# FFN's last 42 inner channels in one output product instead of three, in a one-core attention and FFN kernel

## The reference, cut to what matters

```python
HID = int(DIM * 4 * 2 / 3)          # 682 with DIM = 256
h = shift_token(x)
h = (h - mu) / jnp.sqrt(var + 1e-05) * lg + lb
h = h @ w1 + b1                     # 2 * 682 columns
a, g = jnp.split(h, 2, axis=-1)
h = a * jax.nn.gelu(g, approximate=False)
x = x + h @ w2 + b2                 # 682 rows of w2
```

## Time and profile before

| | |
|---|---|
| median of 3 runs | 1422.95 us (1420.28 to 1424.81) |
| profiled execution, its own time | 1424.29 us |
| its span in the trace | 1422.5 us |
| TensorE busy | 1374.8 us, 97% |
| TensorE weight loads | 1050.5 us, 74% |
| VectorE busy | 963.8 us, 68% |
| ScalarE busy | 878.1 us, 62% |
| GpSimd busy | 762.1 us, 54% |
| chain that ended last | PE 78%, ACT 11%, DVE 5%, issue 4% |

### The profile page before, as it was taken

The page is one execution under the profiler, slowest core; times in us unless marked ns, Lnnn a source line. Parts: engine busy times, 40 slices in busy tenths (PEclk is TensorE's granted clock), DMA queues, the critical chain, the costliest instruction groups (busy, mean ns, idle before and its releaser), DMA issues.

```text
span 1422.5 us, 24115 instructions
## 1 busy us (share of the span) xinstructions
PE 1374.8 (97%) x7740; PEld 1050.5 (74%) x7740; DVE 963.8 (68%) x2671; ACT 878.1 (62%) x2223; POOL 762.1 (54%) x522
## 2 busy tenths in 40 slices
PE   6999997999999999999999999999999999999988
PEld 5878775777777777777777777786777777777756
DVE  6877765767676666666667777676767676766657
ACT  4556656575747575747475766666565757575763
POOL 2425765564647373738373747464655646473710
PEclk9999999999999999999999999999999999999998
DMA  7111100000000000000001010000000000000046
GB/s 220 38 51 60 55 30 1 1 1 0 0 0 0 0 0 0 0 0 0 0 1 60 14 47 1 1 0 0 0 0 0 0 0 0 0 0 0 0 145 210
DMA packets 35243, 33.33 MB, mean 23 GB/s; under 512 B 8364, under 2 KB 32896, under 8 KB 35200
## 3 DMA queue, kind: packets, MB, share of 16 engines
q1 hardware_dynamic: 35200, 32.79, 7.3%
HBM read 24.39 MB, written 8.39 MB: 23 GB/s over the span
## 4 chain that ended last, share of the span: by engine, by line
PE 78%; ACT 11%; DVE 5%; issue 4%; POOL 1%; DMA 0%; ACTq 0%; SPq 0%; DVEq 0%; POOLq 0%
PE l_psF L1399 9%; PE l_psP L842 9%; PE l_ring L842 9%; PE l_ring L1399 8%; PE l_ring L1469 7%; ACT l_att L1073 7%; PE l_psP L1453 6%; PE l_psF L1487 6%; PE l_psS L1410 5%; PE l_psS L1422 4%; PE l_ring L653 3%; PE l_psF L1439 2%; PE l_psS L671 1%; PE l_psP L688 1%; ACT L1163 1%
## 5 line engine op out<-in xcount | busy, mean ns | idle before, releaser
L955 POOL TENSOR_TENSOR l_att<-l_att 128x1024 f32<-128x1024 f32 x64 | 153.1, 2403 | 315.7 <-DVE l_att L880 315.7
L1007 POOL TENSOR_TENSOR l_att<-l_att,l_rinv 128x1024 f32<-128x1024 f32 x64 | 126.4, 1975 | 70.7 <-DVE l_rinv L1243 70.4
L1053 ACT ACTIVATE l_att<-l_psP 128x384 f32<-128x384 f32 (+1 forms) x128 | 70.3, 549 | 120.7 <-PE l_psP L1453 120.4
L1248 DVE COPY l_att<-l_psP 128x384 f32<-128x384 f32 (+1 forms) x128 | 78.9, 617 | 86.7 <-PE l_psP L1453 82.5
L1453 PE MATMUL l_psP<-ident,l_att 128*128 128x128 f32 x896 | 124.5, 279 | 2.0 <-DVE l_att L1248 1.5
L1453 PEld LDWEIGHTS l_psP<-ident,l_att 128*128 128x128 f32 x896 | 98.6, 141 | 32.4 <-issue 28.2
L962 POOL TENSOR_TENSOR l_att<-l_att,l_rn 128x1024 f32<-128x1024 f32 x64 | 120.8, 1910 | 0.7 <-ACT l_rn L861 0.5
L1073 ACT ACTIVATE l_att<-l_psF,l_nb 128x256 f32<-128x256 f32 x256 | 118.1, 483 | 2.1 <-DVE l_nb L1236 2.1
L971 POOL TENSOR_TENSOR l_u_lo<-l_att,l_u_hi 128x512 fp32r<-128x512 f32 x75 | 95.7, 1288 | 39.1 <-ACT l_u_hi L1048 39.0
L1469 PE MATMUL l_ring<-l_att 128*64 128x256 f32 (+1 forms) x1024 | 112.5, 362 | 2.0 <-ACT l_att L1053 1.4
L1236 DVE CUSTOM_DVE_ANT_0 l_psF<-l_psF,w_mask 128x256 f32<-128x256 f32 x256 | 101.1, 456 | 16.3 <-issue 16.3
(11 more groups left out here) (209 smaller groups left out, 4037.2 us busy)
## 6 DMA issues: line engine op xcount, KB each, us to landing
a_tables<-in_x SPq DMA_DIRECT2D x8, 512.0 KB, 4.3
scratch_s<-a_o SPq DMA_DIRECT2D x8, 512.0 KB, 3.2
l_att<-in_x SPq DMA_DIRECT2D x8, 512.0 KB, 8.8
l_att<-scratch_s SPq DMA_DIRECT2D x8, 512.0 KB, 9.0
out_dram<-l_att SPq DMA_DIRECT2D x7, 512.0 KB, 7.8
aw_stage<-in_wqkv SPq DMA_DIRECT2D x2, 768.0 KB, 5.9
l_att<-in_wqkv SPq DMA_DIRECT2D x2, 768.0 KB, 5.4
w_w_raw<-in_w SPq DMA_DIRECT2D x2, 640.0 KB
```

The costliest lines, as they stand in the source:

```text
L955: pool.tensor_tensor(rot[:, t, :], rot[:, t, :], t2[t % 2], ALU.add).then_inc(S["added"], 1)
L1007: pool.tensor_tensor(pr, pr, along(inv, 2 * P), ALU.mult).then_inc(S["p_done"], 1)
```

## The change

Tile 5 of the FFN has only 42 inner channels, and its operands have 128 rows. The change fills the rows with the parts of the split, so that one product gives all three. With AGAIN = 10 (channels 32 to 41), the rows are, for the hidden values: 0 to 41 high parts; 42 to 51 and 52 to 61 channels 32 to 41 again, as low and as high parts; 64 to 95 low parts of channels 0 to 31; 96 to 127 high parts of channels 0 to 31 again. The rows of w2 are laid out to match (high, high, low; high; low). The columns of w1 and the entries of b1 for channels 32 to 41 are loaded two more times, so that the hidden product itself makes the copies.

```diff
 load_w1, for each half s:
+            for r in range(2):
+                c1 = c + HREM + r * AGAIN
+                sp.dma_start(stage[:, :, c1:c1 + AGAIN], w1[:, :, (s + 1) * HID - AGAIN:(s + 1) * HID]).then_inc(self.S["w1_in"], 16)
 load_w2:
-        sp.dma_start(self.w2_raw[0:HREM, HFULL, :], self.io["w2"][layer, HFULL * P:HID]).then_inc(self.S["w2_in"], 16)
+        for p0, first, n in ((0, 0, HREM), (HREM, 32, AGAIN), (HREM + AGAIN, 32, AGAIN), (64, 0, 32), (96, 0, 32)):
+            row = HFULL * P + first
+            sp.dma_start(self.w2_raw[p0:p0 + n, HFULL, :], self.io["w2"][layer, row:row + n]).then_inc(self.S["w2_in"], 16)
 load_small:
+        sp.dma_start(self.less[:, :], io["fless"]).then_inc(small, 16)
 and for each layer l and half s:
+                for r in range(2):
+                    p0 = s * GATE0 + HREM + r * AGAIN
+                    sp.dma_start(self.b1col[p0:p0 + AGAIN, l, 2 * HFULL:W1T], rest[32:HREM], allow_slow_non_contiguous=True).then_inc(small, 16)
 low_w2 covers tiles 0 to 4 only; new:
+    def end_w2(self, dve, layer):
+        end = (slice(0, P), HFULL)
+        dve.wait_ge(self.S["small"], self.SMALL)
+        dve.wait_ge(self.S["w2_hi"], layer + 1)
+        dve.scalar_tensor_tensor(out=self.w2_hi[end], in0=self.w2_hi[end].bitcast(F32), scalar=self.less[:, 1:2], in1=self.w2_raw[end],
+                                 op0=ALU.mult, op1=ALU.add).then_inc(self.S["w2_end"], 1)
 ScalarE, u_high (gelu and gated now cover rows 0 to 63 instead of 0 to 41):
+            if j == HFULL:
+                act.activation(U_hi[96:P, j, :], gate_of(j, attn)[0:32, :], ACT.Copy).then_inc(S["u_again"], 1)
 VectorE, u_low of tile 5:
-            dve.tensor_tensor(U_lo[0:rows, j, :], gate_of(j, attn)[0:rows, :], U_hi[0:rows, j, :].bitcast(F32), ALU.subtract).then_inc(low_done(0, j)[0], 1)
+                dve.scalar_tensor_tensor(out=U_hi[32:GATE0, j, :], in0=U_hi[32:GATE0, j, :].bitcast(F32), scalar=W.less[32:GATE0, 0:1],
+                                         in1=u[32:GATE0, :], op0=ALU.mult, op1=ALU.add)
+                dve.tensor_tensor(U_hi[64:96, j, :], u[0:32, :], U_hi[0:32, j, :].bitcast(F32), ALU.subtract).then_inc(S["u_lo_last"], 1)
 VectorE, end of step 0:
-                for half in (U_hi, U_lo):
-                    dve.tensor_copy(half[:, HFULL, :], C.zero[:, :].broadcast_to([P, N]))
+                W.end_w2(dve, 0)
 VectorE, end of step 8:
                 W.low_w2(dve, 1)
+                W.end_w2(dve, 1)
 TensorE, down:
+                    if k == HFULL:
+                        ge(pe, S["u_again"], i)
+                        pe.wait_ge(WS["w2_end"], l + 1)
-                for m, (w, u) in enumerate(((W.w2_hi, U_hi), (W.w2_hi, U_lo), (W.w2_lo, U_hi))):
+                for m, (w, u) in enumerate(((W.w2_hi, U_hi), (W.w2_hi, U_lo), (W.w2_lo, U_hi))[:1 if k == HFULL else 3]):
```

More of the change, by code:

```diff
@@ L94, in __init__ @@
         self.b2col = sb("b2", [P, LAYERS, KD])
+        self.less = sb("less", [P, 2])
         self.cosT = sb("cos", [P, LAYERS, TT, 2, DH])
@@ L173, in low_wo @@
         dve.tensor_tensor(self.wo_lo[:, :, :], self.wo_raw[:, :, :], self.wo_hi[:, :, :].bitcast(F32), ALU.subtract).then_inc(self.S["wo_lo"], 1)
[L176 to L178 removed]
     def high_w2(self, act, layer):
[L181 to L184, removed]
+        act.wait_ge(self.S["w2_in"], 96 * (layer + 1))
+        act.activation(self.w2_hi[:, :, :], self.w2_raw[:, :, :], ACT.Copy).then_inc(self.S["w2_hi"], 1)
     def low_w2(self, dve, layer):
+        full = slice(0, HFULL)
         dve.wait_ge(self.S["w2_hi"], layer + 1)
[L188 to L190 removed]
+        dve.tensor_tensor(self.w2_lo[:, full, :], self.w2_raw[:, full, :], self.w2_hi[:, full, :].bitcast(F32), ALU.subtract).then_inc(self.S["w2_lo"], 1)
+    def end_w2(self, dve, layer):
[4 more added lines that the diff above has]
+                                 op0=ALU.mult, op1=ALU.add).then_inc(self.S["w2_end"], 1)
 class Shared:
@@ L968, in u_low @@
         def u_low(i, j, attn):
-            rows = P if j < HFULL else HREM
             ge(pool, S["u_hi"], HT * (i - 1) + j + 1)
-            pool.tensor_tensor(U_lo[0:rows, j, :], gate_of(j, attn)[0:rows, :], U_hi[0:rows, j, :].bitcast(F32), ALU.subtract).then_inc(low_done(0, j)[0], 1)
+            pool.tensor_tensor(U_lo[:, j, :], gate_of(j, attn), U_hi[:, j, :].bitcast(F32), ALU.subtract).then_inc(S["u_lo"], 1)
         def step(i, la, lf, last=False):
@@ L1402, in hidden, with down @@
                 last.then_inc(S["w1_ps"], 1)
-        def down(i, c, tiles):
+        def down(i, c, tiles, l):
             for k in tiles:
@@ L1408, in down @@
                     ge(pe, *low_done(i - 1, k))
-                for m, (w, u) in enumerate(((W.w2_hi, U_hi), (W.w2_hi, U_lo), (W.w2_lo, U_hi))):
-                    last = pe.matmul(down_of[c], w[:, k, c * P:(c + 1) * P], u[:, k, :], start=(k == 0 and m == 0), stop=(k == HT - 1 and m == 2))
+                    if k == HFULL:
+                        ge(pe, S["u_again"], i)
+                        pe.wait_ge(WS["w2_end"], l + 1)
+                for m, (w, u) in enumerate(((W.w2_hi, U_hi), (W.w2_hi, U_lo), (W.w2_lo, U_hi))[:1 if k == HFULL else 3]):
+                    last = pe.matmul(down_of[c], w[:, k, c * P:(c + 1) * P], u[:, k, :], start=(k == 0 and m == 0), stop=(k == HFULL))
             if HT - 1 in tiles:
@@ L1507, in step @@
                 ge(pe, S["x_attn"], KD * i)
-                down(i, 0, range(HT))
-                down(i, 1, range(0, 3))
+                down(i, 0, range(HT), lf)
+                down(i, 1, range(0, 3), lf)
                 turned_back(14)
-                down(i, 1, range(3, HT))
+                down(i, 1, range(3, HT), lf)
                 turned_back(15)
@@ L1550, in step @@
                 pe.wait_ge(WS["w2_lo"], lf + 1)
-                down(i, 0, range(0, 4))
+                down(i, 0, range(0, 4), lf)
             if attn:
@@ L1556, in step @@
                     if ffn and u in (2, 4):
-                        down(i, 0, range(3 + u // 2, 4 + u // 2))
+                        down(i, 0, range(3 + u // 2, 4 + u // 2), lf)
                     if u >= 5 and u % 2:
@@ L1564, in step @@
                         ge(pe, S["exp_done"], UNITS * i + UNITS - 1)
-                        down(i, 1, range(0, 3))
+                        down(i, 1, range(0, 3), lf)
                     if ffn and u == UNITS:
-                        down(i, 1, range(3, 5))
+                        down(i, 1, range(3, 5), lf)
                     if ffn and u == UNITS + 1:
-                        down(i, 1, range(5, HT))
+                        down(i, 1, range(5, HT), lf)
                 pe.wait_ge(WS["wo_lo"], la + 1)
@@ L1648, in shape_constants @@
     fmask = np.concatenate([prev, own], axis=1)
-    return dict(acos=rows(acos), asin=rows(asin), fcos=rows(fcos), fsin=rows(fsin), amask=amask, fmask=fmask, ident=np.eye(P, dtype=f))
+    p = np.arange(P)
+    less = np.stack([(p >= HREM) & (p < HREM + AGAIN), (p >= HREM + AGAIN) & (p < HREM + 2 * AGAIN) | (p >= 96)], axis=1)
+    fless = np.where(less, f(-1), f(0))
+    return dict(fless=fless, acos=rows(acos), asin=rows(asin), fcos=rows(fcos), fsin=rows(fsin), amask=amask, fmask=fmask, ident=np.eye(P, dtype=f))
 NAMES = dict(x="L0_attn_x", wq="L0_attn_w_q", wk="L0_attn_w_k", wv="L0_attn_w_v", wqkv="L0_ffn_wqkv", q_scale="L0_ffn_q_scale",
```

31 lines of the change are left out of this document (16 added, 15 removed).

## The result

The changed kernel takes 1481.96 us (median of 4 runs, 1480.06 to 1485.87), the kernel before 1423.88 us beside it (4 runs, 1420.28 to 1425.93): ratio 1.042, 95% interval [1.0404, 1.0436], so 58 us or 4.2% slower. Forecast were 1455 us and at most 1460. The profiled execution took 1480.06 us with a span of 1478.3, 55.8 us more than that of before.

The account below looks back on a forecast made before the run. In the softmax stretch, TensorE, ScalarE and VectorE hand tiles to each other, so waits count more than TensorE's matmuls. VectorE +30.6, set-up +2.3 and -0.6 gave +32.3 us: 1455 us, range 1429 to 1460.

Parts of the forecast that it names:

- The clock falls: Rival: TensorE's new pause in each step lowers its clock, 15 x 1 to 2 us on top: 1470 to 1485; chance 0.04.
- VectorE's lock: Softmax stretch: tile 5's second VectorE instruction waits for GpSimd's scaling; transposes of unit 1 2.04 us late, +30.6 us.
- the order at the port: Tile 5's pair: GpSimd takes the port between VectorE's two instructions, at 671.93, and holds it to 673.82.
- The lower end: Softmax stretch: with VectorE's second instruction not blocked, the transposes of unit 1 start at 674.96, +0.41 us a step.
- Port is no obstacle: Rival: VectorE keeps the port for its pair, or the two share it; +7.9 us, 1430.8; chance 0.13.
- Matmuls removed: FFN's second product: 64 fewer matmuls, 14.7 us of TensorE time, 0.47 us at each of two places a step.
- c=0: Output half whose tile 5 matmuls precede 674.55: 0.47 us a step saved if nothing else comes late; two things do.
- c=1: Output half before unit 7's transposes at 692.71, which already wait 0.2 us for VectorE's evacuation of unit 6: 0 saved.
- Set-up: Loads: 12 more ahead of batch 2's input, +2.3 us once (0 to 3.5); GpSimd's shorter low part of w2, -0.6 us.
- Tail: Last step: 4 matmuls fewer, but VectorE and TensorE arrive together at the last sum: 0, at most -0.1 us.

Follow-up runs that it names:

- e1_fill: Changed kernel plus seven 512-column matmuls per step in TensorE's pause ahead of the transposes of unit 1, output unchanged: 1462.22 us, ratio 1.0287.
- e6_pair_first: Changed kernel with VectorE's two tile 5 instructions moved ahead of the reciprocal that lets GpSimd start scaling unit 1: 1439.10 us, ratio 1.0124.
- e2_psum: Changed kernel with tile 5's product u left in PSUM, so each of VectorE's two instructions has one SBUF operand: 1438.34 us, ratio 1.0113.
- e4_before_scalar: Kernel before plus a second ScalarE copy (32 rows x 512) behind tile 5's copy in the 15 middle steps: 1434.93 us, ratio 1.0089.
- k1_both: s1_late_w2 with ScalarE's second copy of tile 5 behind the exponentials of unit 2, reading from SBUF: 1424.28 us, ratio 1.0011.
- e5_before_fewer: Kernel before with tile 5's two other products left out (64 matmuls less, output lacks those low parts): 1420.36 us, ratio 0.9985.
- f1_filler: e2_psum with the tiles of output half c=1 dealt out as 2, 2 and 2 instead of 3, 2 and 1: 1427.26 us, ratio 1.0035.
- h_before_order: Kernel before with the tiles of output half c=1 dealt out as 2, 2 and 2 instead of 3, 2 and 1: 1419.33 us, ratio 0.9982.
- g2_early_evac: f1_filler with tile 5's second copy, VectorE subtraction and c=0 matmul moved later, and unit 0's evacuation inside unit 3's minimum search: 1428.69 us, ratio 1.0040.
- s1_late_w2: f1_filler with the six w2 loads issued three batches before the first stage's end, not ahead of batch 2's input load: 1423.64 us, ratio 1.0013.
- e3_before_vector: Kernel before plus one VectorE subtraction (32 rows x 512, both operands in SBUF) ahead of tile 5's low part, 15 middle steps: 1468.23 us, ratio 1.0324.

## Why the prediction was wrong

**The clock: the step that failed.** Step "The clock falls" of the rivals had 0.04, with "Against: with the pauses that the stretch has now it is 1.00". That is no argument against a pause that the stretch does not have now: in the kernel before TensorE never idles over 0.6 us in it. The forecast itself put a pause of 2 us there, and the tail stood in the earlier trace rows with 0.88. The cases were taken as exclusive, while this one comes on top of the forecast. With the forecast's 1455 and its own 15 x 1 to 2 us it gave 1470 to 1485, and the result is 1482. Measured, the stretch has 0.90 or 0.91 in 13 of 15 steps, it makes 12 of them 1.6 us longer (the last has a clock of 0.94 behind its stretch, before 0.91), and e1_fill gives 20 us back. The range ended at 1460 because it left these 20 us out. They are most of the miss, not all of it: e1_fill, with the clock at 1.00, is still 2 us above the range, by the sizes below, and part of why the rival's 1470 to 1485 fits is that the lock was taken too small.

**VectorE's lock: right in kind, short in size.** The instruction, the engine, the order at the port and the 0.55 us after its release came as written in the steps in which the second instruction waits: the transposes are 2.32 us late there, 2.04 were said. The rest is small terms: the pair starts 0.12 us later in the step, its first instruction takes 0.74 us instead of 0.65, so GpSimd too is later, and the minima start 0.04 us after the pair, where 0.04 us ahead was assumed. In 10 of 15 steps it is the first instruction that waits, which the forecast did not have; there the transposes are 2.46 us late. The two steps without the clock's fall are 2.4 us longer, which would be 36.5 us in 15 steps; e1_fill has 34.9, in place of 30.6.

The Trainium skill (SBUF — State Buffer, Who interferes with whom) has the engine that issues first hold the shared ports for its whole instruction, and the second to issue blocked fully. The trace agrees that the block is full: 2.48 us for an instruction that takes 0.74 us in e6_pair_first, ending 0.54 us after GpSimd. On who is first it agrees in five steps; in the other ten the blocked VectorE instruction has the earlier recorded start, by 0.04 us.

**The lower end.** "Port is no obstacle" was priced at 0.41 us a step. With the lock out of the way (e2_psum, e6_pair_first) it is 0.71 to 0.76. ScalarE's second copy was taken at 0.52 us and adds 0.79 from copy to exponential (e4_before_scalar), and the pair makes 0.71 where the copy no longer stands ahead (k1_both).

**Matmuls removed: right that they are worth little.** But "0.47 us is saved if nothing else comes late" for c=0 was too much: VectorE's evacuation of unit 0 ends at 674.17, so without any addition 0.21 us are saved (e5_before_fewer). For c=1, as it is placed, nothing is, as forecast. That c=1's idle could be bought back by moving filler (f1_filler) was not looked for.

**Set-up.** +1.7 us was said; the profile after shows +0.14, and the term is there all the same. That the load of batch 2 was forecast to land at 38.4 and was read at 39.41 is luck: w2 has 4 more loads and not 3, the 13 new loads keep the queue 3.7 us longer and not 12 x 0.55, and the load lands 7.8 us after its issue and not the median 4.3; it took 7.6 before too, which is up to the moment at which VectorE read it. It is issued at 31.56 instead of 28.47. Its issue and VectorE's reading of it after:

```profile
31.56 0.41 SPq L351 DMA_DIRECT2D a_tables<-in_x  x1
...
39.41 1.41 DVE L532 BATCH_NORM_STATS2 a_stats<-a_tables 128x6 f32<-128x256 f32 x4 [2.05 <-DMA a_tables<-in_x]
```

VectorE waits 2.05 us and reads it 3.3 us later than before. What hides it, as far as single profiled executions can tell, is the clock in the first attention step, from 220 to 255 us: 0.90 before, 1.00 after (the first row is of before):

```profile
220.00:255.00 35.00, 28.50 (x195) 20.14 (x196) 18.94 (x85) 19.18 (x71) 13.98 (x12) 0.90 0.00 1
...
220.00:255.00 35.00, 26.63 (x207) 19.10 (x204) 20.54 (x94) 20.64 (x77) 16.39 (x14) 1.00 0.01 1
```

Of kernels with the old set-up, h_before_order has 1.00 there and its first GELU of tile 5 at 291.85, 1.9 us ahead of before. Of those with the new one, after, e1_fill and f1_filler have 1.00 and 293.93 to 294.78, and e6_pair_first, g2_early_evac and e2_psum have 0.90 and 297.18 to 298.62. Like with like, set-up costs 2.1 to 2.9 us at 1.00 and 3.4 to 4.8 us at 0.90 (against before's 293.79). Why it is more at 0.90 was not found. s1_late_w2 gives 3.6 us back.

**Tail:** 0 was said, +0.2 us from the last GELU to the end.

## What to carry to other kernels

Where VectorE and GpSimd hold each other up, count instructions and not their work: one more short instruction with two SBUF operands, placed where GpSimd starts one of 1.9 us, made a step 2.2 us longer (e3_before_vector) even with the clock at 1.00, and an operand in PSUM or a place ahead of what starts GpSimd took that away. When a forecast opens a pause on TensorE, price the clock on top of it and not as a case beside it. Removing matmuls that serve as filler was worth 2 of 14.7 us until the ones that are left were dealt out to the waits that need them, and where two engines end together at the next hand-over, a saving on one alone was not seen (k1_both).

## What the runs showed of the hardware

The length of the pauses alone does not tell whether the clock falls: in the changed kernel pauses of 0.86, 0.18 and 1.74 us are followed by a stretch at 1.00 in 2 steps and at 0.90 or 0.91 in 8 of the same execution (the 5 steps without the 0.18 have 0.90), and pauses of 0.77 and 1.17 us by 0.90 in 9 of 15. With 0.77 and 0.33 us (e2_psum), or 1.10 us alone (k1_both), it did not fall in any step. What decides between like steps was not found.

The order of the recorded starts does not settle who goes first when they lie this close. VectorE starts 0.04 us ahead of GpSimd (612.27, 612.31) and ends only 0.54 us after it, 1.74 us late; it starts 0.05 us ahead (690.44, 690.49) and goes first. One SBUF operand beside a PSUM one took no part in the lock in any of the 15 steps of e2_psum.
